# Cross attention with a scan on one core: row maxima taken over every fourth query and moved to rows by DMA, and the output projection run three groups ahead

## The chip, the cores and the metric

The kernel runs on one core of a Trainium2 chip. The metric is the device time of one execution in microseconds; the kernel before takes 2360.32 us, the median of 3 runs (2359.78 to 2363.59).

## What is computed

One transformer block with 4096 queries (x, 512 features) and 3202 keys (ctx), all in fp32. Cut to what matters:

```python
x  = layernorm(builder_state, g1, beta1)
kv = layernorm(base_state, g1, beta1)
q, k, v = heads of x @ Wq.T + bq, kv @ Wk.T + bk, kv @ Wv.T + bv      # 8 heads of 64
out = softmax(q @ k.T / 8) @ v
x = builder_state + out @ W_o.T + b_o
U = (layernorm(x, g2, beta2) @ W_in.T + b_in) @ Bmat
s = silu(s @ A.T) + u_t          # for every t, giving states
x = x + states @ Cmat
return x + (program_probs.mean(axis=1) @ W_prog.T + b_prog)
```

## The kernel before

Five engines each run a list of instructions written out by hand; semaphores join them. PE does the matmuls, ScalarE the exponentials and copies, VectorE the maxima and sums from PSUM, GpSimd (POOL) sums of the exponentials, and SP issues almost all DMAs, in one queue that also waits. On SP a wait holds up every DMA behind it.

**Precision.** q, k, O and W_o are split into a high part in fp32r and a low part, and a product is three passes. The maxima use the high parts alone.

**Stages.** Projection of q to DRAM (`q_scratch`) and of k and v, to 325 us; the attention, to 2121 us; the output projection with the second layernorm and U, to 2284 us; the scan and its output, to 2359 us.

**The attention** is cut into 32 units, one for each block of 512 queries and each pair of heads (`unit(w)`). A unit has 26 tiles of 128 keys, taken two at a time in 13 steps (`j`). In a step PE does, in this order: one of the maxima of a later unit (line 1136 or 1141); the shift for the even tile, a matmul of `ones_row` with `sh` (line 1230); the scores of both tiles (lines 1238, 1240, 1242); a second one of the maxima; PV of the two tiles before (line 1263). Every matmul here is a pair, one on the upper and one on the lower 64 rows of the array (or columns, for PV), for the two heads; the two run together. The shift subtracts the row maximum before the exponential. The even tile gets it on PE, the odd one on VectorE, which adds `shb` to PSUM (line 959).

**The maxima.** `maxima(w, m, i)` multiplies 128 queries of `qh` (the stationary operand) with 512 keys, so that a query is a partition and VectorE can reduce over the keys (`take_max`, lines 886 and 889). A unit has 26 of them: 24 with 512 keys, and two with the last 130 keys of two query tiles each (line 1141). `maxima_of` deals them out: 34 in unit 0, then two in a step, so that those of unit u + 1 end in step 8 of unit u. `row_max` (line 896) then reduces them to one maximum for each query and head in `mxp`. But `sh` and `shb` want the maxima along the free dimension. So PE transposes `mxp` in four pieces (`turn_max`, line 1150) in step 9, ScalarE copies the two rows, negated, to `sh` (`shift`, line 676), and SP stores them to `m_scratch` and loads them from there to all partitions of `shb` (`spread_shift`, lines 353 and 356).

**The output projection** has 16 groups of 256 queries. `project(d, t)` (line 1327) multiplies a tile of `og`, loaded by SP (`load_og`), with `wo_hl`, into bank 2 + t of PSUM; VectorE adds `xb` and takes the layernorm's statistics (`project` on VectorE), ScalarE normalises into `xn` (`norm2`), PE transposes (`turn2`, line 1336) and multiplies with `w_u` (`finish`, line 1348). PE runs two groups ahead: it projects group d + 2 before it transposes group d. `og` has two slots. The last unit's O goes through this stage late: its sum over keys (`spread_sum`, `take_den`, `fold_den`, `invert`, `spread_rden`), its scaling (`scale_o`, `high_o`, `low_o`) and its store (`store_o`) stand between the groups, and SP waits for each of them in its one queue. Groups 14 and 15 need that O.

**The scan** (line 1384) has as its moving operand `su` at every sixteenth column.

## Time and profile before

| | |
|---|---|
| median of 3 runs | 2360.32 us |
| the profiled execution | 2361.04 us |
| its span | 2358.9 us |
| PE busy | 2280.1 us, 97% |
| weight loads (PEld) busy | 1322.0 us, 56% |
| VectorE, GpSimd, ScalarE busy | 73%, 67%, 48% |
| share of PE in the chain that ended last | 91% |
| granted clock of PE over the execution | 0.978 |

In the views of the trace, PE stands for matmuls and PEld for the loads of their stationary operands, which can run beside a matmul before them. A form such as 64*128 64x512 is a matmul on 64 rows and 128 columns of the array, with 512 columns streamed. Matmuls are pipelined, so that the sum of their durations is more than the time in which PE is busy. SPq is SP issuing a DMA, and the time beside it is the time to issue it, not to move the data.

### The profile page before, as it was taken

What the parts mean: (1) busy time and instruction counts of PE and PEld (TensorE: products, weight loads), DVE (VectorE), ACT (ScalarE), POOL (GpSimd) and SP (SyncE); (2) the same over time, 40 slices, a digit from 0 to 9 for tenths busy, and PEclk for the clock granted to TensorE, in tenths of its full rate; (3) what the DMA queues carried; (4) which work ended last, traced back from release to release, by engine and by line L of the source; (5) the groups of instructions that cost most, each with busy time, mean ns of one, the idle gap of its engine ahead of it and who ended that gap; (6) DMA issues with size and microseconds to landing.
All of it is one profiled execution on the core that took longest, in us unless ns stands there. A gap on an engine that the chain in (4) does not pass through costs nothing.

```text
span 2358.9 us, 35969 instructions
## 1 busy us (share of the span) xinstructions
PE 2280.1 (97%) x14148; PEld 1322.0 (56%) x14148; DVE 1726.2 (73%) x2167; ACT 1121.5 (48%) x1429; POOL 1583.0 (67%) x1039
## 2 busy tenths in 40 slices
PE   8999989999999999999999999999999999998787
PEld 8998854555555545555555555555555555446553
DVE  5865446888888878888888878888877888646645
ACT  3654424444444444444544445444445444542354
POOL 1200026888888888888888888888888888883211
PEclk8999989999999999999999999999999999999887
DMA  6650225677777777777777777667777776775623
GB/s 242 216 175 10 81 75 120 151 156 157 157 154 160 169 168 171 174 156 159 164 161 166 178 171 166 154 154 155 160 157 157 156 159 155 183 175 152 198 77 143
DMA packets 158678, 365.01 MB, mean 155 GB/s; under 512 B 22511, under 2 KB 62063, under 8 KB 157870
## 3 DMA queue, kind: packets, MB, share of 16 engines
q0 software_dynamic: 59904, 218.13, 45.3%
q1 hardware_dynamic: 98606, 144.58, 18.9%
q8 instruction: 112, 1.84, 0.3%
q14 instruction: 56, 0.46, 0.1%
HBM read 95.41 MB, written 49.02 MB: 61 GB/s over the span
## 4 chain that ended last, share of the span: by engine, by line
PE 91%; DMA 3%; DVE 3%; ACT 1%; issue 1%; POOL 1%; SPq 0%; ACTq 0%; DVEq 0%; POOLq 0%
PE ps L1263 32%; PE ps L1136 11%; PE ps L1238 8%; PE ps L1240 8%; PE ps L1242 8%; PE ps L1230 4%; PE ps L1100 4%; PE ps L1118 3%; PE ps L1108 3%; PE ps L1327 3%; DMA acca<-pt 2%; PE ps L1384 1%; PE ps L1081 1%; PE ps L1273 1%; DVE mx_part L886 1%
## 5 line engine op out<-in xcount | busy, mean ns | idle before, releaser
L702 ACT ACTIVATE pt<-ps 128x1024 f32<-128x1024 f32 x800 | 779.2, 1021 | 911.5 <-PE ps L1242 889.5
L886 DVE TENSOR_REDUCE mx_part<-ps 128x2 f32<-128x1024 f32 x768 | 938.6, 1222 | 350.9 <-PE ps L1136 350.9
L520 POOL TENSOR_TENSOR accp<-accp,pt 128x1024 f32<-128x1024 f32 x416 | 1035.8, 2490 | 236.3 <-ACT pt L702 233.0
L1263 PE MATMUL ps<-pt,v 128*64 128x512 f32 x3328 | 807.0, 606 | 0.0
L959 DVE TENSOR_TENSOR ps<-ps,shb 128x1024 f32<-128x1024 f32 x403 | 493.2, 1224 | 50.5 <-PE ps L1242 50.5
L1263 PEld LDWEIGHTS ps<-pt,v 128*64 128x64 f32 x3328 | 202.2, 136 | 345.7 <-issue 338.5
L1136 PE MATMUL ps<-kk,qh 64*128 64x512 f32 x1536 | 350.6, 451 | 9.6 <-DVE mx_part L886 9.6
L1136 PEld LDWEIGHTS ps<-kk,qh 64*128 64x128 f32 x1536 | 143.6, 184 | 367.6 <-DVE mx_part L886 267.3
L1238 PE MATMUL ps<-qh,kk 64*128 64x512 f32 x1664 | 330.0, 391 | 3.9 <-ACT pt L702 3.9
L1242 PE MATMUL ps<-ql,kk 64*128 64x512 f32 x1664 | 330.1, 390 | 0.0
L1240 PE MATMUL ps<-qh,kk 64*128 64x512 f32 x1664 | 330.0, 391 | 0.0
L530 POOL DMA_DIRECT2D acca<-pt x192 | 182.3, 950 | 3.3 <-ACT pt L702 2.0
L1238 PEld LDWEIGHTS ps<-qh,kk 64*128 64x128 f32 x1664 | 157.8, 185 | 38.9 <-ACT pt L702 5.8
L1240 PEld LDWEIGHTS ps<-qh,kk 64*128 64x128 f32 x1664 | 158.4, 185 | 34.5
L1242 PEld LDWEIGHTS ps<-ql,kk 64*128 64x128 f32 x1664 | 158.4, 185 | 34.1
L1230 PE MATMUL ps<-sh,ones_row 64*128 64x512 f32 x858 | 173.9, 401 | 0.9 <-ACT pt L702 0.9
L509 POOL MEMSET sh<- 128x512 f32 x2 | 1.0, 530 | 187.2 <-PE ps L1118 187.2
L540 POOL DMA_DIRECT2D accb<-pt x128 | 125.7, 982 | 0.1
L1327 PE MATMUL ps<-wo_hl,og 128*128 128x512 f32 x384 | 100.0, 417 | 25.8 <-DMA og<-o_scratch 24.8
L1327 PEld LDWEIGHTS ps<-wo_hl,og 128*128 128x128 f32 x384 | 75.5, 201 | 48.2 <-DMA og<-o_scratch 27.0
L565 POOL TENSOR_TENSOR xb<-xb,bo 128x512 f32<-128x512 f32 x32 | 40.6, 1319 | 84.2 <-DMA xb<-x 84.2
L1230 PEld LDWEIGHTS ps<-sh,ones_row 64*128 64x128 f32 x858 | 82.6, 187 | 15.0 <-ACT pt L702 12.3
(150 smaller groups left out, 1933.5 us busy)
## 6 DMA issues: line engine op xcount, KB each, us to landing
acca<-pt POOLq DMA_DIRECT2D x224, 512.0 KB, 4.9
accb<-pt POOLq DMA_DIRECT2D x160, 512.0 KB, 4.8
q_scratch<-kk SPq DMA_DIRECT2D x32, 512.0 KB, 4.5
acca<-accp POOLq DMA_DIRECT2D x32, 512.0 KB, 4.6
o_scratch<-ost SPq DMA_DIRECT2D x32, 512.0 KB, 3.0
og<-o_scratch SPq DMA_DIRECT2D x32, 512.0 KB, 5.5
shb<-m_scratch SPq DMA_DIRECT2D x31, 512.0 KB, 4.2
xs<-x SPq DMA_DIRECT2D x16, 512.0 KB, 6.3
```

Source lines behind the costliest of these rows:

```text
L520: nc.gpsimd.tensor_tensor(acc[:, :], acc[:, :], pt[n % PT_SLOTS][:, :], ALU.add).then_inc(added_p, 1)
L530: nc.gpsimd.dma_start(acc[:, :], pt[n % PT_SLOTS][:, :], accum_op=ALU.add).then_inc(added_a[u % 2], 16)
L702: nc.scalar.activation(pt[n % PT_SLOTS][:, :], src, ACT.Exp, scale=SCALE).then_inc(exped, 1)
L886: nc.vector.tensor_reduce(mx_part[:, m % QT, :, m // QT], src, AX_X, ALU.max).then_inc(max_taken, 1)
L959: nc.vector.tensor_tensor(ps[:, b:b + 2, :], ps[:, b:b + 2, :], shb[u % 2][:, :, :], ALU.add)\
L1136: ins = mm(ps[:, bank, :], q[r, (m % QT) * P:(m % QT + 1) * P], kk[r, p, 0, a:a + QB], start=True, stop=True)
L1230: ins = mm(ps[:, 2 * (t % 2) + h, :], ones_row[r, :], sh[u % 2][r, :], start=first, stop=not first)
L1238: mm(ps[:, b + h, :], kk[r, p, 0, key], qh[u % 3][r, :], start=first, stop=False)
L1240: mm(ps[:, b + h, :], kk[r, p, 1, key], qh[u % 3][r, :], start=False, stop=False)
L1242: ins = mm(ps[:, b + h, :], kk[r, p, 0, key], ql[u % 2][r, :], start=False, stop=last)
L1263: ins = mm(ps[HD * h:HD * (h + 1), 6, :], v[:, t, f:f + HD], pt[n % PT_SLOTS][:, h * QB:(h + 1) * QB], start=(t == 0), stop=(t == NT - 1))
L1327: ins = mm(ps[:, 2 + t, :], og[:, d % 2, a, k, rows], wo_hl[:, b, k], start=(i == 0), stop=(i == len(PASSES) - 1))
```

## The change

It has two parts.

1. The maxima of `maxima(w, m, i)` are over queries `m % 4`, `m % 4 + 4`, ... (`q[r, m % QT:QB:QT]`) and no longer over 128 neighbouring ones; so partition p holds queries 4p to 4p + 3. For units 1 to 31 `row_max` writes a tile `mx_row` of 128 x 2 x 4, a second VectorE instruction negates it to `shift_col`, and SP stores that to `m_scratch` (each partition two pieces of 16 bytes), loads two rows of it into `sh`, and then `shb` as before. The transposes and ScalarE's copy stay for unit 0 only.
2. The output projection runs three groups ahead and `og` has three slots. The work on the last unit's O moves: on PE, ScalarE earlier (`spread_sum` and `take_den` at d = 0 for 2, `high_o` at 6 for 8), on GpSimd later (`scale_o` 10 for 8, `low_o` 12 for 10), on SP later (`fold_den` 6 for 4, `spread_rden` 9 for 6, `store_o` 13 for 10). The third slot lies where `wo_raw` was, so that its first load waits for `bo_mm` and `wo_lo`.

```diff
             def spread_shift(w):
                 sp.wait_ge(shift_ready, w + 1)
-                sp.dma_start(m_scratch[w % 2], sh[w % 2][0:HD + 1:HD, :].bitcast(F32)).then_inc(sh_stored, 16)
+                sp.dma_start(m_scratch[w % 2].rearrange("h (p t) -> p h t", t=QT), shift_col[:, :, :].bitcast(F32))\
+                    .then_inc(sh_stored, 16)
                 sp.wait_ge(sh_stored, 16 * w)
+                sp.dma_start(sh[w % 2][0:HD + 1:HD, :].bitcast(F32), m_scratch[w % 2]).then_inc(sh_loaded, 16)
                 wait(sp, shifted, tiles_added(w - 1))
...
             for d in range(2, X_G):
-                sp.wait_ge(y_done, GT * (d - 1))
-                if d % 2 == 0:
-                    sp.wait_ge(o_stored, 16 * (UNITS - BLOCKS + d // 2 + 1))
-                load_og(d)
+                if d >= OG_SLOTS:
+                    sp.wait_ge(y_done, GT * (d - OG_SLOTS + 1))
+                    if d % 2 == 0:
+                        sp.wait_ge(o_stored, 16 * (UNITS - BLOCKS + d // 2 + 1))
+                    load_og(d)
                 sp.wait_ge(x1_ready, GT * (d - 1))
                 load_x2(d)
-                if d == 4:
+                if d == 6:
                     fold_den(UNITS - 1)
-                if d == 6:
-                    spread_rden(UNITS - 1)
...
-                if d == 10:
+                if d == 9:
+                    spread_rden(UNITS - 1)
+                if d == 13:
                     store_o(UNITS - 1)
...
             def row_max(w):
                 dve.wait_ge(max_taken, NM * (w + 1))
-                wait(dve, max_turned, w)
-                nc.vector.tensor_reduce(mxp[:, :, 0:HD + 1:HD], mx_part[:, :, :, :], AX_X, ALU.max).then_inc(max_ready, 1)
-
+                wait(dve, sh_stored, 16 * (w - 1))
+                nc.vector.tensor_reduce(mx_row[:, :, :], mx_part[:, :, :, :].rearrange("p t h k -> p h t k"), AX_X, ALU.max).then_inc(max_ready, 1)
+                dve.wait_ge(max_ready, w + 1)
+                nc.vector.tensor_scalar(shift_col[:, :, :], mx_row[:, :, :], -1.0, None, ALU.mult).then_inc(shift_ready, 1)
...
-                        ins = mm(ps[:, bank, :], q[r, (m % QT) * P:(m % QT + 1) * P], kk[r, p, 0, a:a + QB],
+                        ins = mm(ps[:, bank, :], q[r, m % QT:QB:QT], kk[r, p, 0, a:a + QB],
                                  start=True, stop=True)
...
-                            ins = mm(ps[:, bank, i * TAIL_N:(i + 1) * TAIL_N], q[r, qt * P:(qt + 1) * P],
+                            ins = mm(ps[:, bank, i * TAIL_N:(i + 1) * TAIL_N], q[r, qt:QB:QT],
                                      kk[r, p, 0, TAIL:KEYS], start=True, stop=True)
...
-                if t == 0:
-                    pe.wait_ge(shift_ready, u + 1)
+                if t == 0 and u == 0:
+                    pe.wait_ge(shift_ready, 1)
+                if t == 0 and u > 0:
+                    pe.wait_ge(sh_loaded, 16 * u)
...
-                    if ahead and j == turn_step(u):
-                        turn_max(u + 1)
...
-                if d + 2 < X_G:
-                    project(d + 2, 1)
+                if d + OG_SLOTS < X_G:
+                    project(d + OG_SLOTS, 1)
                 turn2(d)
-                if d == 2:
+                if d == 0:
                     spread_sum(UNITS - 1)
```

PE's order in step 9 of a unit before, from the scores of the even tile on (line 1238, 1240, 1242 are the passes of the scores; 1150 the transposes, 1136 a maximum, 1263 PV):

```order
L1230 MATMUL ps<-sh_69,ones_row 128x512 x2
L1238 MATMUL ps<-qh_65,kk 128x512 x2
L1240 MATMUL ps<-qh_65,kk 128x512 x2
L1242 MATMUL ps<-ql_67,kk 128x512 x2
L1238 MATMUL ps<-qh_65,kk 128x512 x2
L1240 MATMUL ps<-qh_65,kk 128x512 x2
L1242 MATMUL ps<-ql_67,kk 128x512 x2
L1150 MATMUL ps<-ident,mxp 65x128 x4
L1136 MATMUL ps<-kk,qh_64 128x512 x2
L1263 MATMUL ps<-pt_71,v 64x512 x2
```

The same place in the changed kernel, whose lines are some nine further down:

```order
L1239 MATMUL ps<-sh_69,ones_row 128x512 x2
L1247 MATMUL ps<-qh_65,kk 128x512 x2
L1249 MATMUL ps<-qh_65,kk 128x512 x2
L1251 MATMUL ps<-ql_67,kk 128x512 x2
L1247 MATMUL ps<-qh_65,kk 128x512 x2
L1249 MATMUL ps<-qh_65,kk 128x512 x2
L1251 MATMUL ps<-ql_67,kk 128x512 x2
L1144 MATMUL ps<-kk,qh_64 128x512 x2
L1272 MATMUL ps<-pt_71,v 64x512 x2
```

The four transposes are gone and the maximum follows the scores directly, as in every other step.

SP's queue for one unit before (the denominators of the unit before, the shifts of the next unit, the store of O):

```order
L361 DMA den_80<-den_sb 64x1x8 x2
L366 DMA r_scratch<-rden_81 128x8
L370 DMA rdenb<-r_scratch 64x512 x2
L353 DMA m_scratch<-sh_69 2x512
L356 DMA shb_83<-m_scratch 128x1024
L413 DMA o_scratch<-ost 128x2x512
```

and in the changed kernel:

```order
L362 DMA den_80<-den_sb 64x1x8 x2
L367 DMA r_scratch<-rden_81 128x8
L371 DMA rdenb<-r_scratch 64x512 x2
L352 DMA m_scratch<-shift_col 128x2x4
L355 DMA sh_69<-m_scratch 2x512
L357 DMA shb_83<-m_scratch 128x1024
L414 DMA o_scratch<-ost 128x2x512
```

The store has another form, and the load of `sh` stands between it and the load of `shb`.

PE's order at the start of the output projection before:

```order
L1327 MATMUL ps<-wo_hl,og 128x512 x72
L1336 MATMUL ps<-ident,xn 128x128 x8
L1327 MATMUL ps<-wo_hl,og 128x512 x24
L1336 MATMUL ps<-ident,xn 128x128 x8
L1327 MATMUL ps<-wo_hl,og 128x512 x12
L1348 MATMUL ps<-nt,w_u 64x256 x8
```

and in the changed kernel:

```order
L1333 MATMUL ps<-wo_hl,og 128x512 x96
L1342 MATMUL ps<-ident,xn 128x128 x8
L1281 MATMUL ps<-acca_87,ones 64x512 x2
L1333 MATMUL ps<-wo_hl,og 128x512 x24
L1342 MATMUL ps<-ident,xn 128x128 x8
L1333 MATMUL ps<-wo_hl,og 128x512 x12
```

Four groups are projected before the first transposes in place of three (24 matmuls are a group), and the sum of the last unit follows these transposes directly.

## Rows read from the trace of the kernel before

**Rows 1.** The page, part 1: busy time of each engine.

```profile
PE 2280.1 (97%) x14148; PEld 1322.0 (56%) x14148; DVE 1726.2 (73%) x2167; ACT 1121.5 (48%) x1429; POOL 1583.0 (67%) x1039
```

**Rows 2.** Windows by stage: us, busy of PE, PEld, DVE, ACT, POOL, clock, DMA, GB/s.

```profile
383.00:2050.00 1667.00, 1661.87 (x10470) 848.40 (x10468) 1338.78 (x1226) 818.60 (x897) 1402.81 (x895) 1.00 0.72 161
2121.00:2284.00 163.00, 132.07 (x648) 100.28 (x648) 97.96 (x312) 57.42 (x98) 49.38 (x39) 0.91 0.49 154
```

**Rows 3.** Windows of two steps, PE alone, the first with the transposes.

```profile
1212.29:1217.22 4.93, 4.93 (x33) 1.00 0.74 138
1217.22:1221.35 4.13, 4.13 (x28) 1.00 0.60 156
```

**Rows 4.** Timeline of the weight loads in a step: start, length in us.

```profile
1204.06 0.19 PEld L1136 LDWEIGHTS ps<-kk,qh 64*128 64x128 f32 x2 [0.81 <-DVE mx_part L886]
1204.17 0.19 PEld L1230 LDWEIGHTS ps<-sh,ones_row 64*128 64x128 f32 x2
...
1205.55 0.19 PEld L1242 LDWEIGHTS ps<-ql,kk 64*128 64x128 f32 x2
1205.88 0.19 PEld L1136 LDWEIGHTS ps<-kk,qh 64*128 64x128 f32 x2
```

**Rows 5.** Timeline of VectorE in that unit.

```profile
1204.60 1.23 DVE L886 TENSOR_REDUCE mx_part<-ps 128x2 f32<-128x1024 f32 x1 [0.54 <-PE ps L1136]
...
1211.53 0.21 DVE L896 TENSOR_REDUCE mxp<-mx_part 128x8 f32<-128x56 f32 x1
1212.90 1.23 DVE L886 TENSOR_REDUCE mx_part<-ps 128x2 f32<-128x1024 f32 x1 [1.15 <-PE ps L1136]
```

**Rows 6.** Timeline of the weight loads, the last step of a set.

```profile
1208.21 0.30 PEld L1141 LDWEIGHTS ps<-kk,qh 64*128 64x128 f32 x4 [0.81 <-DVE mx_part L886]
...
1209.91 0.43 PEld L1141 LDWEIGHTS ps<-kk,qh 64*128 64x128 f32 x4
```

**Rows 7.** Windows in the scan, columns as in rows 2.

```profile
2290.00:2295.00 5.00, 4.84 (x19) 2.41 (x18) 0.00 (x0) 3.33 (x10) 0.00 (x0) 0.50 0.00 0
2315.00:2320.00 5.00, 4.84 (x19) 1.70 (x18) 3.02 (x5) 3.40 (x9) 0.00 (x0) 1.00 0.00 0
```

**Rows 8.** Groups of 2315:2320 us (first row), then single lines (min/median/max ns).

```profile
L1384 PE MATMUL ps<-su,at_sb 128*64 128x128 f32 x19 | 5.1, 398 | 0.2
...
L1348 PE MATMUL ps<-nt,w_u x128: 379/379/687, 2151.9 to 2283.8; 128*64 128x256 f32 x128
...
L1336 PE MATMUL ps<-ident,xn x128: 270/272/475, 2140.3 to 2279.7; 128*128 128x128 f32 x128
...
L1018 DVE TENSOR_REDUCE cb_sum<-cb_sb x1: 2931/2931/2931, 2227.1 to 2227.1; 128x64 f32<-128x1664 f32 x1
```

**Rows 9.** The page, part 5: busy, mean ns, idle before and releaser.

```profile
L1327 PE MATMUL ps<-wo_hl,og 128*128 128x512 f32 x384 | 100.0, 417 | 25.8 <-DMA og<-o_scratch 24.8
```

**Rows 10.** Timeline of SP, the shifts of one unit.

```profile
1216.89 0.51 SPq L353 DMA_DIRECT2D m_scratch<-sh  x1
1218.49 0.33 SPq L356 DMA_DIRECT2D shb<-m_scratch  x1
```

**Rows 11.** The page, part 6: KB each, us from issue to landing.

```profile
og<-o_scratch SPq DMA_DIRECT2D x32, 512.0 KB, 5.5
```

**Rows 12.** Timeline of PE in the output projection.

```profile
2165.93 8.22 PE L1327 MATMUL ps<-wo_hl,og 128*128 128x512 f32 x24 [7.21 <-DMA og<-o_scratch]
...
2187.66 7.33 PE L1327 MATMUL ps<-wo_hl,og 128*128 128x512 f32 x24 [4.18 <-DMA og<-o_scratch]
...
2230.20 8.53 PE L1327 MATMUL ps<-wo_hl,og 128*128 128x512 f32 x24 [9.42 <-DMA og<-o_scratch]
...
2248.20 5.72 PE L1327 MATMUL ps<-wo_hl,og 128*128 128x512 f32 x24
...
2278.14 1.97 PE L1336 MATMUL ps<-ident,xn 128*128 128x128 f32 x8 [3.64 <-ACT xn L743]
```

**Rows 13.** Timeline of SP in the output projection.

```profile
2160.56 1.14 SPq L418 DMA_DIRECT2D og<-o_scratch  x2
```

More of the change, by code:

```diff
@@ L32 @@
 X_SLOTS = 8
+OG_SLOTS = 3
 QB = 512
@@ L199, in build @@
         mxp = at("mxp", [P, QT, HD + 1], RR + 11776)
+        mx_row = at("mx_row", [P, 2, QT], 2576)
+        shift_col = at("shift_col", [P, 2, QT], 2584, F32R)
         mx_part = at("mx_part", [P, QT, 2, 7], RR + 12040)
@@ L298, in build @@
         bvb_ready = sem("bvb_ready"); bo_mm = sem("bo_mm"); bo_ready = sem("bo_ready")
-        og_loaded = [sem("og_loaded_0"), sem("og_loaded_1")]; x2_loaded = [sem("x2_loaded_0"), sem("x2_loaded_1")]
+        og_loaded = [sem(f"og_loaded_{i}") for i in range(OG_SLOTS)]; x2_loaded = [sem("x2_loaded_0"), sem("x2_loaded_1")]
         xb_ready = sem("xb_ready"); y_done = sem("y_done"); x1_ready = sem("x1_ready")
@@ L587, in _ @@
                 add_bias(d)
-                if d == 8:
+                if d == 10:
                     scale_o(UNITS - 1)
-                if d == 10:
+                if d == 12:
                     low_o(UNITS - 1)
@@ L669, in _, with first_shift @@
                     high_k(g, 3)
-            def shift(w):
-                act.wait_ge(max_turned, w + 1)
-                if w == 0:
-                    act.wait_ge(ones_set, 3)
-                nc.scalar.activation(sh[w % 2][0:HD + 1, :], ps[0:HD + 1, 7, :], ACT.Copy, scale=-1.0)\
-                    .then_inc(shift_ready, 1)
+            def first_shift():
+                act.wait_ge(max_turned, 1)
+                act.wait_ge(ones_set, 3)
+                nc.scalar.activation(sh[0][0:HD + 1, :].rearrange("r (p t) -> r p t", t=QT),
+                                     ps[0:HD + 1, 7, :].rearrange("r (t p) -> r p t", t=QT), ACT.Copy, scale=-1.0)                    .then_inc(shift_ready, 1)
             def exp_tile(u, t):
@@ L717, in high_o @@
                 nc.scalar.activation(ost[:, 0], oraw[:, :], ACT.Copy).then_inc(o_hi, 1)
-            shift(0)
+            first_shift()
             for u in range(UNITS):
@@ L729, in _ @@
                         high_o(u - 1)
-                    if j == turn_step(u) and u + 1 < UNITS:
-                        shift(u + 1)
                     if u == UNITS - 2 and j in (3, 5, 7, 9):
@@ L1140, in maxima, with first_turn @@
                             qt = 2 * (m - (NM - 2)) + i
-                            ins = mm(ps[:, bank, i * TAIL_N:(i + 1) * TAIL_N], q[r, qt * P:(qt + 1) * P],
+                            ins = mm(ps[:, bank, i * TAIL_N:(i + 1) * TAIL_N], q[r, qt:QB:QT],
                                      kk[r, p, 0, TAIL:KEYS], start=True, stop=True)
                 ins.then_inc(max_done, 1)
-            def turn_max(w):
-                pe.wait_ge(max_ready, w + 1)
-                wait(pe, den_taken, w - 1)
+            def first_turn():
+                pe.wait_ge(max_ready, 1)
                 for q in range(QT):
@@ L1269, in spread_sum @@
                 pe.wait_ge(added_a[u % 2], 16 * (len(A_TILES) + 1) * (u // 2 + 1))
-                if u + 1 < UNITS:
-                    pe.wait_ge(shift_ready, u + 2)
+                wait(pe, den_taken, u)
                 for h in (0, 1):
@@ L1326, in project @@
                 for i, (k, a, b) in enumerate(PASSES):
-                    ins = mm(ps[:, 2 + t, :], og[:, d % 2, a, k, rows], wo_hl[:, b, k],
+                    ins = mm(ps[:, 2 + t, :], og[:, d % OG_SLOTS, a, k, rows], wo_hl[:, b, k],
                              start=(i == 0), stop=(i == len(PASSES) - 1))
@@ L1353, in _ @@
             pe.wait_ge(bo_ready, 1)
-            for d in (0, 1):
+            for d in range(OG_SLOTS):
                 project(d, 0)
@@ L1357, in _ @@
             for d in range(X_G):
-                if d + 2 < X_G:
-                    project(d + 2, 0)
+                if d + OG_SLOTS < X_G:
+                    project(d + OG_SLOTS, 0)
                 if d > 0 and d % 2 == 0:
                     finish(d // 2 - 1)
-                if d + 2 < X_G:
-                    project(d + 2, 1)
+                if d + OG_SLOTS < X_G:
+                    project(d + OG_SLOTS, 1)
                 turn2(d)
-                if d == 2:
+                if d == 0:
                     spread_sum(UNITS - 1)
-                if d == 9:
+                if d == 8:
                     pe.wait_ge(cb_summed, 1)
```

31 lines of the change are left out of this document (18 added, 13 removed).

## The prediction

> **What bounds the kernel now.** I read the page's busy shares first, then its chain of waits, then windows by stage, then single steps of the attention in the timeline. PE is busy 2280.1 us, 97% of the span [rows 1], and the chain that ended last runs over PE nearly all the time. So time comes off only where PE does less or waits less, and anything that makes PE's own work longer is paid in full. By stage [rows 2]: from 383 to 2050 us (units 1 to 30 of the attention) PE is busy 1661.9 of 1667 us, at full clock: nothing is waited for there. From 2121 to 2284 us (the output projection) it is busy 132 of 163 us, at a granted clock of 0.91: there are some 31 us of waiting. The change touches both stages.
>
> The profiled execution took 2361.04 us, 2.1 more than its span and 0.7 above the median of the three runs (2360.32). The sum is made against 2361.0. I count a change of 0.2% (4.7 us) as the least that a measurement of this kernel tells from none.
>
> **Part 1: the transposes go.** A step with the four transposes lasts 4.93 us, the next one without them 4.13 [rows 3]: 0.80 us for each of 31 units, and since PE is the bound it is all gain: **-24.8 us**. ScalarE's copy into sh goes too; it is worth nothing, as ScalarE is busy 48% of the span [rows 1].
>
> **Part 2: the new way of the maxima.** VectorE gets one more small instruction per unit beside a reduction of 0.21 us, and it then sits idle 1.15 us before its next work [rows 5]: nothing. If that idle time were not there, it would cost 31 x 0.2 = 6 us. On SP's queue the store changes its form (128 partitions x 2 pieces of 16 bytes) and a load of two rows into sh is put between it and the load of shb. In the trace the old store is issued at 1216.89 and SP passes the wait for it at 1218.49, so 1.6 us in all [rows 10]. The new store and the new load are bounded by that 1.6 us below, and above by the 5.5 us of a load of 512 KB [rows 11]: 3 to 11 us together. I take 5. PE wants sh at the start of the next unit, four steps of 4.1 us after the row maximum (at 1211.7): 16 us. So it is in time at either end, and shb with it, since store and load now start at 1212 and not at 1217. Behind that wait on SP stands only the store of O, which was behind one already. Nothing.
>
> **Part 3: every fourth query as the weights.** This is the term that decides. The stationary operand of each matmul for the maxima was 128 consecutive columns of qh; now it is every fourth, 16 bytes apart. No weight load in this trace reads with a step, so its price must be bounded. Lower bound: nothing. Upper bound from the nearest rows: the scan's matmuls (line 1384) stream 128 elements that lie 64 bytes apart. At full clock they take 398 ns on average, where 128 consecutive elements take 272 ns and 256 consecutive ones 379 [rows 8]. And PE finishes 19 of them in 5 us at clock 0.50 and also 19 at clock 1.00 [rows 7], where eight transposes with consecutive operands take 1.97 us at the low clock [rows 12] against half of that at the high one. So a stepped operand of 32 bits seems to come at half the rate, whatever the clock. VectorE shows it too: cb_sum reads 1664 elements 256 bytes apart in 2.93 us, 1.76 ns each [rows 8], against 1.23 us for 1024 consecutive ones, 1.20 ns each [rows 5].
>
> The Trainium skill (SBUF — State Buffer, "Door 1: The DMA port swizzle") speaks against this change: it says that SBUF has lines of 16 bytes, that full rate needs at least two hits in a line, and that each access to a new line pays. Every fourth fp32 is a new line each time. The same paragraph then says that for fp32 a step of 4 is still free. By its first half the term is the one below, by its second half it is zero; the rows above, with far longer steps, cannot part the two at exactly 16 bytes.
>
> I take the upper bound, twice the time, since two engines show it. Now the size. A weight load of 128 columns holds the path for 0.11 us (starts at 1204.06 and 1204.17 [rows 4]); doubled, 0.22. The first load of maxima in a step stands right behind PV, cannot start ahead and is wholly exposed: +0.11. The second starts at 1205.88. The load before it started at 1205.55, and matmul pairs are 0.23 us apart, so its own matmul could start at 1206.01; it would be ready at 1206.10 in place of 1205.99: +0.09, so with the rounding some 0.19 us per step. (It starts where the first reduction, 1204.60 + 1.23, is done [rows 5], and that reduction moves back with the first matmul, so VectorE absorbs none of it.) In the last step of a set there are four loads for short matmuls, 0.30 and 0.43 us [rows 6], nothing to hide behind: +0.44. After the first unit there are 772 maxima, two in a step, so 386 steps: 356 x 0.19 + 30 x 0.44 = 67.6 + 13.2 = 80.8 us. The 34 maxima of unit 0 and 26 in the projections of K add about 60 x 0.09 = 5. **+86 us**, with 0 as the lower end.
>
> **Part 4: the output projection.** PE waits 24.8 us for og there [rows 9]. Three stalls make most of it, and each one leaves the clock low, so that the 24 projections behind it take 8.22, 7.33 and 8.53 us where 5.72 is normal [rows 12]: 6.9 us more. The stalls are not og's own transfer but what stands ahead of it on SP: og is issued at 2160.56 [rows 13] right after SP waited for the denominators of the last unit; the others follow the reciprocals and the store of the last O. The change puts these three later on SP (d = 6, 9, 13 for 4, 6, 10), their producers earlier on PE and ScalarE (d = 0), and gives og a third slot, so that a load of 5.5 us [rows 11] is issued about two loops before PE wants it. Gain 24.8 + 6.9 = 31.7. Against it: the last loops without a projection wait for ScalarE's xn, 3.64 us in the one shown [rows 12]; there is one more such loop: 3.6. Some 2 us for the copies into c1 and c2, which now stand in front of that wait. The bank: project(3, 0) needs VectorE to have emptied project(2, 0), so being three ahead doesn't fill the banks any deeper. I take **-26 us**; between -32 and -15, if one stall of 10 us stays.
>
> **Sum.** 2361.0 - 24.8 + 86 - 26 = **2396 us**.
>
> **Rivals.**
> *A, the forecast: stepped weights at half rate, exposed.* 60%. Its own range, from 70 to 95 us for the term and 18 to 30 for part 4, is 2376 to 2412.
> *B, the stepped load costs nothing* (the line's second-half rule above, or a weight path that fetches ahead). For it: no row shows a step of exactly 16 bytes, nor a stepped weight load. Against: two engines slow down with steps. Then 2361.0 - 24.8 - 26 = 2310 us. This is the faster side; it decides from the point where the term is below 51 us, that is below 0.12 us for a step. 27%.
> *C, half exposed*: only the first load of a step shows, the second hides in the 0.09 us which it now waits for VectorE: 386 x 0.11 + 30 x 0.22 + 3 = 52 us, so 2361.0 + 52 - 51 = 2362 us, no change. 10%.
> *D, the way through DRAM comes late.* If store, load and issue took more than the 16 us, PE would stand at the start of each unit, 31 us for each us too late, on top of any of the above. For it: 256 pieces of 16 bytes, which no row here shows. Against: five us at the least in hand by the bounds above. 3%.
>
> **The numbers.** The likeliest is A, 2396. B alone holds more than 2 in 10, so the range has to reach it: 2308 to 2408. Faster by over 0.2%: B and a little of C, 0.29. Within 0.2%: the middle of C, 0.06. Slower: A, D and the rest of C, 0.65.
>
> **What would show it.** Weight loads of the maxima of some 0.29 us in place of 0.18, steps of 4.3 us in place of 4.13, the same length in every step of a unit but the last of a set (4.5), and PE still busy without a gap: A. Loads of 0.18 us and steps of 4.13 throughout: B, and I am wrong by 86 us. For part 4: no wait over 2 us for og, the clock high throughout, the stage 137 us long in place of 163. If og is still waited for, the third slot was not what was short. For D: PE idle before the first shift matmul of a unit, released by the load of sh.

## The result and the profile after

The changed kernel takes **2445.48 us** (median of 4 runs, 2442.4 to 2447.16) beside 2360.05 us for the kernel before on the same chip: a ratio of 1.0358 [1.0345, 1.0371], 85 us slower. The forecast was 2396 with a range of 2308 to 2408. The direction was right and the size was not: 49 us more than forecast, 37 us above the upper end of the range.

| | before | after |
|---|---|---|
| span of the profiled execution | 2358.9 | 2443.7 |
| attention | 1797.1 | 1881.5 |
| output projection | 163.4 | 161.5 |
| a usual step of the attention | 4.13 to 4.15 | 4.36 to 4.37 |
| granted clock over the execution | 0.978 | 0.977 |

The attention runs from its first matmul to the first one of the output projection (323.76 to 2120.83 us, and 325.82 to 2207.33), the output projection from there to the end of its last matmul. The attention took 84.4 us more, what stands before it 2.1 more, the output projection 1.9 less, the scan 0.2 more: 84.8, all of the span's growth.

The page of the changed kernel, parts 1 and 4, to be read beside [rows 1]:

```profile
PE 2361.2 (97%) x14024; PEld 1415.7 (58%) x14024; DVE 1790.0 (73%) x2198; ACT 1110.4 (45%) x1398; POOL 1580.9 (65%) x1039
...
PE 87%; DVE 8%; issue 2%; ACT 1%; DMA 1%; POOL 0%; SPq 0%; ACTq 0%; POOLq 0%; DVEq 0%
PE ps L1272 29%; PE ps L1144 14%; PE ps L1247 7%; PE ps L1251 7%; PE ps L1249 7%; PE ps L1108 4%; PE ps L1239 4%; PE ps L1126 3%; PE ps L1116 3%; PE ps L1333 2%; DVE mx_part L889 2%; DVE shift_col L905 2%; PE ps L1390 1%; DVE ps L967 1%; PE ps L1089 1%
```

PE has 124 matmuls fewer (31 x 4 transposes) and is busy 81 us longer, with 94 us more of weight loads. That is the forecast mechanism. But VectorE now holds 8% of the chain, and one line of it is `shift_col L905`, a negation of 8 elements per partition, which the forecast had priced at nothing. It stands on the chain with 2% of the span.

Windows of the changed kernel, columns as in [rows 2]. The first three are one step each, from one first shift matmul to the next: the last of a set of maxima, the step behind the row maximum, a usual one. The fourth is the output projection.

```profile
1195.77:1200.17 4.40, 4.40 (x31) 2.71 (x32) 3.85 (x5) 1.94 (x2) 3.10 (x3) 1.00 0.84 181
1200.17:1205.23 5.06, 4.64 (x28) 2.34 (x26) 4.39 (x4) 2.05 (x2) 3.93 (x3) 1.00 0.65 118
1205.23:1209.60 4.37, 4.37 (x28) 2.34 (x26) 3.49 (x3) 2.46 (x3) 3.69 (x4) 1.00 0.74 195
2207.33:2368.85 161.52, 134.37 (x650) 100.55 (x648) 104.71 (x312) 57.64 (x98) 49.59 (x39) 0.91 0.52 156
```

In the second window a step that has lost its four transposes lasts 5.06 us, longer than the 4.93 that it took with them [rows 3]. PE is idle 0.42 us in it (5.06 less the 4.64 busy).

**The loads.** Timeline of the weight loads in two places of that unit (start, length, and the idle time before with what ended it):

```profile
1202.35 0.31 PEld L1144 LDWEIGHTS ps<-kk,qh 64*128 64x128 f32 x2 [0.85 <-DVE mx_part L889]
...
1204.77 0.31 PEld L1144 LDWEIGHTS ps<-kk,qh 64*128 64x128 f32 x2 [0.81 <-DVE mx_part L889]
1204.97 0.21 PEld L1239 LDWEIGHTS ps<-sh,ones_row 64*128 64x128 f32 x2
1205.23 0.19 PEld L1247 LDWEIGHTS ps<-qh,kk 64*128 64x128 f32 x2
```

The load of the maxima takes 0.31 us where it took 0.19, and the next one starts 0.20 us behind it where it started 0.11 behind [rows 4]: the path is held for twice as long. Loads of consecutive columns (L1247) still take 0.19.

**The negation.** Timeline of VectorE and, in the second fence, of GpSimd around the row maximum:

```profile
1198.83 0.21 DVE L903 TENSOR_REDUCE mx_row<-mx_part 128x8 f32<-128x56 f32 x1
1199.07 2.10 DVE L905 TENSOR_SCALAR shift_col<-mx_row 128x8 fp32r<-128x8 f32 x1
1201.08 1.21 DVE L889 TENSOR_REDUCE mx_part<-ps 128x2 f32<-128x1024 f32 x1
```

```profile
1198.77 2.37 POOL L526 TENSOR_TENSOR accp<-accp,pt 128x1024 f32<-128x1024 f32 x1 [1.30 <-ACT pt L707]
1201.09 0.86 POOL L536 DMA_DIRECT2D acca<-pt  x1
```

The negation starts at 1199.07 and ends at 1201.17; GpSimd's running sum, begun 0.30 us before it, ends at 1201.14. The reduction of the same 128 x 8 outputs right before it took 0.21 us while the same sum was running. The next reduction of maxima is thereby held until 1201.08, and PE's next maximum waits for the bank until 1202.35: the load of it waits the 0.85 us above, and PE itself is idle for 0.42 of them. Of the 31 negations 30 take 2.09 or 2.10 us. The view of this line gives the shortest, the median and the longest in ns:

```profile
L905 DVE TENSOR_SCALAR shift_col<-mx_row x31: 171/2095/2098, 382.4 to 2133.3; 128x8 fp32r<-128x8 f32 x31
```

The one of 171 ns is the first, and it is the one that no sum stood beside. GpSimd's sum before it ends at 382.34, and the negation starts 0.07 us later:

```profile
379.97 2.37 POOL L526 TENSOR_TENSOR accp<-accp,pt 128x1024 f32<-128x1024 f32 x1 [3.13 <-ACT pt L707]
```

```profile
382.41 0.17 DVE L905 TENSOR_SCALAR shift_col<-mx_row 128x8 fp32r<-128x8 f32 x1
```

The Trainium skill (SBUF — State Buffer, "SBUF: two separate sides") has the mechanism: VectorE and GpSimd share one pair of ports as an exclusive lock, which a VectorE instruction takes in its two-port mode or, beside a GpSimd instruction that reads SBUF, when both its inputs are in SBUF, and whichever engine comes second is blocked for the whole instruction of the other. By that rule the negation can't end before GpSimd's instruction does, and the trace agrees: it ends 0.03 us behind it. In which mode an instruction ran is in no view.

**The output projection.** PE's groups there in the changed kernel, beside [rows 9] (busy, mean ns, idle before, releasers):

```profile
L1333 PE MATMUL ps<-wo_hl,og 128*128 128x512 f32 x384 | 99.4, 416 | 19.7 <-DVE x_first L1010 11.5 <-DVE x_last L1010 8.2
```

Nothing waits for `og` any more. 24.8 us of waiting for a DMA has become 19.7 us of waiting for VectorE's sum into x. Why VectorE is late is in three timelines of the changed kernel, of ScalarE, VectorE and PE:

```profile
2238.89 1.51 ACT L746 ACTIVATE xn<-x_first,small 128x512 f32<-128x512 f32 x2
```

```profile
2235.84 1.35 DVE L1010 TENSOR_TENSOR x_first<-ps,xb 128x512 f32<-128x512 f32 x2
2240.50 1.28 DVE L852 BATCH_NORM_STATS2 small<-x_first 128x6 f32<-128x512 f32 x2 [3.30 <-ACT xn L746]
```

```profile
2223.09 13.38 PE L1333 MATMUL ps<-wo_hl,og 128*128 128x512 f32 x48 [4.59 <-DVE x_first L1010]
...
2246.44 2.97 PE L1333 MATMUL ps<-wo_hl,og 128*128 128x512 f32 x12 [1.53 <-DVE x_first L1010]
...
2264.19 4.44 PE L1333 MATMUL ps<-wo_hl,og 128*128 128x512 f32 x12 [2.74 <-DVE x_first L1010]
...
2283.45 2.96 PE L1333 MATMUL ps<-wo_hl,og 128*128 128x512 f32 x12 [2.66 <-DVE x_first L1010]
...
2301.91 4.57 PE L1333 MATMUL ps<-wo_hl,og 128*128 128x512 f32 x12 [3.44 <-DVE x_last L1010]
```

VectorE has the sum of a group at 2237.2, but starts its statistics only at 2240.50, when ScalarE's `xn` of an older group has ended (2240.40). Behind them stands the next group's sum, which is what empties the bank for PE. The reason is a wait that the change left alone: the layernorm's scale and bias have two slots, so `project(d)` on VectorE waits for `normed2` of group d - 2 before it may write them. PE now runs three groups ahead, so that normalisation has itself to wait for transposes that stand behind a projection on PE. And after some of these waits the granted clock is low: 12 matmuls take 4.44 or 4.57 us there, at a granted clock of 0.63, where others take 2.97 and 2.96, at 1.00.

### The profile page after: what moved, and what is told of

It is laid out like the page before. It is cut to its first block, busy times and chain, and to the rows that moved or that the text cites. A ratio compares the mean times of both kernels' runs of the same rounds, so it can differ in the third digit from the quotient of the medians.

```text
span 2443.7 us, 35692 instructions
## 1 busy us (share of the span) xinstructions
PE 2361.2 (97%) x14024; PEld 1415.7 (58%) x14024; DVE 1790.0 (73%) x2198; ACT 1110.4 (45%) x1398; POOL 1580.9 (65%) x1039
## 4 chain that ended last, share of the span: by engine, by line
PE 87%; DVE 8%; issue 2%; ACT 1%; DMA 1%; POOL 0%; SPq 0%; ACTq 0%; POOLq 0%; DVEq 0%
PE ps L1272 29%; PE ps L1144 14%; PE ps L1247 7%; PE ps L1251 7%; PE ps L1249 7%; PE ps L1108 4%; PE ps L1239 4%; PE ps L1126 3%; PE ps L1116 3%; PE ps L1333 2%; DVE mx_part L889 2%; DVE shift_col L905 2%; PE ps L1390 1%; DVE ps L967 1%; PE ps L1089 1%
## 5 line engine op out<-in xcount | busy, mean ns | idle before, releaser
L526 POOL TENSOR_TENSOR accp<-accp,pt 128x1024 f32<-128x1024 f32 x416 | 1024.8, 2463 | 320.8 <-ACT pt L707 318.8
L1144 PEld LDWEIGHTS ps<-kk,qh 64*128 64x128 f32 x1536 | 237.4, 306 | 386.9 <-DVE mx_part L889 290.4
L1144 PE MATMUL ps<-kk,qh 64*128 64x512 f32 x1536 | 435.8, 563 | 21.8 <-DVE mx_part L889 21.8
L1247 PE MATMUL ps<-qh,kk 64*128 64x512 f32 x1664 | 330.9, 393 | 0.6 <-ACT pt L707 0.6
L1247 PEld LDWEIGHTS ps<-qh,kk 64*128 64x128 f32 x1664 | 157.9, 185 | 35.4 <-ACT pt L707 1.2
L546 POOL DMA_DIRECT2D accb<-pt x128 | 118.7, 927 | 0.0
L1333 PE MATMUL ps<-wo_hl,og 128*128 128x512 f32 x384 | 99.4, 416 | 19.7 <-DVE x_first L1010 11.5
L1239 PEld LDWEIGHTS ps<-sh,ones_row 64*128 64x128 f32 x858 | 89.6, 205 | 16.0 <-ACT pt L707 14.1
```

The source lines that it names most:

```text
L526: nc.gpsimd.tensor_tensor(acc[:, :], acc[:, :], pt[n % PT_SLOTS][:, :], ALU.add).then_inc(added_p, 1)
L1144: ins = mm(ps[:, bank, :], q[r, m % QT:QB:QT], kk[r, p, 0, a:a + QB], start=True, stop=True)
L1239: ins = mm(ps[:, 2 * (t % 2) + h, :], ones_row[r, :], sh[u % 2][r, :], start=first, stop=not first)
L1247: mm(ps[:, b + h, :], kk[r, p, 0, key], qh[u % 3][r, :], start=first, stop=False)
L1333: ins = mm(ps[:, 2 + t, :], og[:, d % OG_SLOTS, a, k, rows], wo_hl[:, b, k], start=(i == 0), stop=(i == len(PASSES) - 1))
```

## The experiments

All kernels below compute the whole output. The kernel before was run beside each; its median was between 2360.1 and 2363.0 us.

**1. Each part alone.** First, part 2 of the change in the kernel before (three slots of `og`, three groups ahead, the moved steps), and no part 1:

```diff
+OG_SLOTS = 3
...
-        og = at("og", [P, 2, 2, FC, GW], 6656, F32R)
+        og = at("og", [P, OG_SLOTS, 2, FC, GW], 6656, F32R)
...
             def project(d, t):
-                pe.wait_ge(og_loaded[d % 2], 32 * (d // 2 + 1))
+                pe.wait_ge(og_loaded[d % OG_SLOTS], 32 * (d // OG_SLOTS + 1))
```

> The kernel before with part 2 of the change alone (three groups ahead, three slots for og, the last unit's O moved); maxima as before. Theory 1 (the stepped weight loads, the negation on VectorE and a projection that gained nothing together make the loss): from the traces the projection lasts 161.5 us in the changed kernel against 163.4 before, so 2361 - 2 = 2359 us, no change; no wait for og, but seven or eight waits of 1.4 to 4.6 us for VectorE's sum into x. Theory 2 (the projection did gain the 26 us that I forecast, and the maxima cost all the more): 2335 us.

Measured: 2357.02 us (10 runs), ratio 0.9983 [0.9973, 0.9993]. Its profile has the waits of the changed kernel, in the same places:

```profile
L1333 PE MATMUL ps<-wo_hl,og 128*128 128x512 f32 x384 | 98.1, 412 | 17.3 <-DVE x_first L1008 12.6 <-DVE x_last L1008 4.6
```

So the second part is worth 3 us, not 26. What it removes is there (no wait for `og`), and is given back.

Second, part 1 alone (the changed kernel with its output projection put back):

```diff
-OG_SLOTS = 3
...
-        og = at("og", [P, OG_SLOTS, 2, FC, GW], 6656, F32R)
+        og = at("og", [P, 2, 2, FC, GW], 6656, F32R)
...
-                if d == 0:
+                if d == 2:
                     take_den(UNITS - 1)
```

> The kernel before with part 1 of the change alone; projection as before. Theory 1: 2445.5 + 2 = 2447 us, steps of 4.37 us, 5.06 in the step after the maxima of a unit. Theory 2: 2445.5 + 26 = 2471 us.

Measured: 2450.92 us, ratio 1.0384 [1.0366, 1.0401], with steps of 4.37 and 5.06 us as in the changed kernel. The parts add up to within 3 us: -3 and +91 against +85. (Put on top of the first part, the second is worth 5 us by the medians and 1 by the spans, 2444.9 and 2443.7.)

**2. The loads alone.** The kernel before, with only the stationary operand of the maxima changed and ScalarE's copy putting the rows back in order; transposes and everything else stay:

```diff
-                nc.scalar.activation(sh[w % 2][0:HD + 1, :], ps[0:HD + 1, 7, :], ACT.Copy, scale=-1.0)\
+                nc.scalar.activation(sh[w % 2][0:HD + 1, :].rearrange("r (p t) -> r p t", t=QT),
+                                     ps[0:HD + 1, 7, :].rearrange("r (t p) -> r p t", t=QT), ACT.Copy, scale=-1.0)\
...
-                        ins = mm(ps[:, bank, :], q[r, (m % QT) * P:(m % QT + 1) * P], kk[r, p, 0, a:a + QB],
+                        ins = mm(ps[:, bank, :], q[r, m % QT:QB:QT], kk[r, p, 0, a:a + QB],
```

> The kernel before with nothing changed but the queries of a maximum (every fourth) and, to match, the order in which ScalarE's copy reads the transposed maxima. Theory 1: weight loads of 0.31 us, steps of 4.37 us, 386 x 0.23 + 34 x 0.1 + 2 = 94 us more than before: 2454. By my forecast's size (0.19 for a step, 86 in all): 2446. Rival (part of the loss of the changed kernel that I put down to the loads comes with the way through DRAM): under 2430.

Measured: 2451.96 us, ratio 1.0384 [1.0365, 1.0402], span 2450.6. Group and windows (a step with the transposes, a usual one):

```profile
L1137 PEld LDWEIGHTS ps<-kk,qh 64*128 64x128 f32 x1536 | 237.3, 306 | 367.2 <-DVE mx_part L887 266.2
```

```profile
1203.30:1208.45 5.15, 5.15 (x34) 2.75 (x31) 3.59 (x3) 2.42 (x3) 4.03 (x3) 1.00 0.63 119
1208.45:1212.81 4.36, 4.36 (x28) 2.34 (x26) 3.49 (x3) 2.46 (x3) 3.62 (x4) 1.00 0.64 173
```

The span grows by 91.7 us from the loads alone; the reordered copy on ScalarE takes 590 ns for 592. And the two windows price the transposes under stepped loads: 5.15 - 4.36 = 0.79 us, as in the kernel before (0.80).

**3. The negation in another form.** My first reading of the 2.10 us was that the one-input instruction's fast mode takes the lock and an instruction with two tensor inputs would not. So -2m + m in place of -1 times m:

```diff
-                nc.vector.tensor_scalar(shift_col[:, :, :], mx_row[:, :, :], -1.0, None, ALU.mult).then_inc(shift_ready, 1)
+                nc.vector.scalar_tensor_tensor(out=shift_col[:, :, :], in0=mx_row[:, :, :], scalar=-2.0,
+                                               in1=mx_row[:, :, :], op0=ALU.mult, op1=ALU.add).then_inc(shift_ready, 1)
```

> The changed kernel with the negation written as a scalar_tensor_tensor (-2 * m + m) in place of a tensor_scalar of one operand. Theory 1 (the tensor_scalar stands until GpSimd's running sum is done, as the other tensor_scalars do in the output projection, and the two-operand form does not): the instruction takes 0.2 us and not 2.1, the step after it 4.37 us and not 5.06, so 2445.5 - 31 x 0.7 = 2424 us. Rival (VectorE waits for something else there, such as the store on SP or the write before): the instruction or the one behind it still takes 2 us, and the time stays at 2445.

Measured: 2446.1 us, ratio 1.0362 [1.0345, 1.0379], the same as the changed kernel.

```profile
1200.61 2.08 DVE L905 SCALAR_TENSOR_TENSOR shift_col<-mx_row 128x8 fp32r<-128x8 f32 x1
```

GpSimd's sum in this run started at 1200.30 and took 2.37, so it ended at 1202.67; the negation ended at 1202.69. That reading fell: one tensor input or two, the negation stands until GpSimd's end. The second case of the Trainium skill's rule above, two inputs in SBUF, fits this run as its first fits the changed kernel.

**4. No negation.** The reduction, which took 0.21 us beside the same GpSimd instruction, writes `shift_col` itself; the sign moves into the constants (`ones_row` is -1, VectorE subtracts `shb`). The rest is the changed kernel.

```diff
-                nc.vector.tensor_reduce(mx_row[:, :, :], mx_part[:, :, :, :].rearrange("p t h k -> p h t k"), AX_X, ALU.max).then_inc(max_ready, 1)
-                dve.wait_ge(max_ready, w + 1)
-                nc.vector.tensor_scalar(shift_col[:, :, :], mx_row[:, :, :], -1.0, None, ALU.mult).then_inc(shift_ready, 1)
+                nc.vector.tensor_reduce(shift_col[:, :, :], mx_part[:, :, :, :].rearrange("p t h k -> p h t k"), AX_X, ALU.max).then_inc(max_ready, 1)
...
-                nc.vector.tensor_tensor(ps[:, b:b + 2, :], ps[:, b:b + 2, :], shb[u % 2][:, :, :], ALU.add)\
+                nc.vector.tensor_tensor(ps[:, b:b + 2, :], ps[:, b:b + 2, :], shb[u % 2][:, :, :], ALU.subtract)\
```

> The changed kernel without the negation: the reduction of the row maxima writes shift_col itself, ones_row holds -1, and VectorE subtracts shb in place of adding it. Theory 1 (both tensor_scalar and scalar_tensor_tensor on SBUF stand until GpSimd's running sum ends, a tensor_reduce does not): the reduction takes 0.21 us, the step behind it 4.37 us in place of 5.06, so 2445.5 - 31 x 0.7 = 2424 us. Rival (the next maxima wait there for another reason, the write of shift_col or its store): the step stays at 5.06 and the time at 2445.

Measured: 2427.68 us, ratio 1.0278 [1.026, 1.0297]: 18 us less than the changed kernel (21 by the spans). The view of the reduction, and windows of the step behind the row maximum and of the next:

```profile
L903 DVE TENSOR_REDUCE shift_col<-mx_part x31: 210/211/211, 384.4 to 2117.2; 128x8 fp32r<-128x56 f32 x31
```

```profile
1194.23:1198.66 4.43, 4.43 (x28) 2.34 (x26) 3.49 (x3) 1.94 (x2) 3.31 (x3) 1.00 0.66 117
1198.66:1203.03 4.37, 4.37 (x29) 2.34 (x26) 3.49 (x3) 2.46 (x3) 4.36 (x4) 1.00 0.71 187
```

5.06 became 4.43 and PE has no idle time in it: 31 x 0.63 = 19.5 us. The negation was the missing term of part 2.

**5. Consecutive queries, so no stepped loads.** The changed kernel with 128 neighbouring queries again; the store to DRAM then falls into 1024 pieces of 4 bytes.

```diff
-                sp.dma_start(m_scratch[w % 2].rearrange("h (p t) -> p h t", t=QT), shift_col[:, :, :].bitcast(F32))\
+                sp.dma_start(m_scratch[w % 2].rearrange("h (t p) -> p h t", t=QT), shift_col[:, :, :].bitcast(F32),
+                             allow_slow_non_contiguous=True)\
...
-                        ins = mm(ps[:, bank, :], q[r, m % QT:QB:QT], kk[r, p, 0, a:a + QB],
+                        ins = mm(ps[:, bank, :], q[r, (m % QT) * P:(m % QT + 1) * P], kk[r, p, 0, a:a + QB],
```

> The changed kernel with the maxima over 128 consecutive queries again; the maxima still go to rows by DMA, in 1024 pieces of 4 bytes in place of 256 of 16. Theory 1 (the step of 16 bytes doubles the weight load): loads of 0.18 us and not 0.31, steps of 4.14 us, so 2445.5 - 386 x 0.23 = 2357 us, if the small pieces land in the 16 us that there are. Rival (the way through DRAM or its traffic slows the steps): the time stays over 2430 or grows with the smaller pieces; should the store come too late, PE waits at the start of each unit, 31 us for each us.

Measured: 2384.8 us, ratio 1.0108 [1.0089, 1.0127]. The loads are back at 183 ns and a usual step at 4.15 us, 61 us less than the changed kernel, but 28 more than I expected. Windows of the step behind the row maximum and of the next, and the group of ScalarE's exponentials from 383 to 2050 us in this run (first fence) and in the changed kernel (second):

```profile
1162.86:1167.93 5.07, 4.42 (x30) 2.10 (x27) 4.63 (x4) 2.05 (x2) 4.18 (x3) 1.00 1.11 129
1167.93:1172.08 4.15, 4.15 (x28) 2.13 (x26) 3.49 (x3) 2.32 (x3) 3.49 (x4) 1.00 0.73 29
...
L707 ACT ACTIVATE pt<-ps 128x1024 f32<-128x1024 f32 x737 | 723.0, 1022 | 864.3 <-PE ps L1251 781.2 <-DMA acca<-pt 60.8 <-DVE ps L967 20.4
```

```profile
L707 ACT ACTIVATE pt<-ps 128x1024 f32<-128x1024 f32 x711 | 694.6, 1022 | 888.8 <-PE ps L1251 871.4 <-DVE ps L967 13.3 <-DMA acca<-pt 4.1
```

Two things make up most of the rest. The wait for GpSimd costs more where steps are shorter: 5.07 - 4.15 = 0.92 us, 29 us in all, for the 21 that I had expected. And the store stands in the way of other DMAs: moving 4 KB, it is issued at 1164.13 and SP passes the wait for it at 1172.89, 8.8 us; in the second window, which lies in that stretch, no more than 29 GB/s are moved (194 in the like window of experiment 6, below). GpSimd's accumulating DMAs (`acca<-pt` in part 6 of the page) land after 5.3 us for 4.8, and ScalarE waits 60.8 us for them for 4.1. These are not SP's: SP does not issue almost all DMAs, as said of the kernel before; GpSimd issues 416 there, with 218 of the 365 MB. The changed kernel's longer steps give them more time; in the kernel before, with steps of the same length, ScalarE waits 14.2. PE waits 14.1 us for ScalarE, 11 more than before (2.7). Together 29 + 11 on 2361.0 - 24.8 - 2 give 2374, against 2380.4 for the profiled execution and 2384.8 for the median: 6 to 11 us stay open. The first negation of this run started 0.42 us before the end of GpSimd's sum (376.28) and took 0.45.

**6. Every second query.** From experiment 4, with a step of 8 bytes: a tile of 128 queries is every second one of 256. The store has 512 pieces of 8 bytes. Were the price that of a step as such, the loads would stay near 0.3 us; were it that of one element in 16 bytes, they would be free.

```diff
-                        ins = mm(ps[:, bank, :], q[r, m % QT:QB:QT], kk[r, p, 0, a:a + QB],
+                        ins = mm(ps[:, bank, :], q[r, 2 * P * (m % QT // 2) + m % 2:2 * P * (m % QT // 2 + 1):2], kk[r, p, 0, a:a + QB],
```

> As no_negation, but a tile holds every second query (steps of 8 bytes, two to a line of 16), and the maxima go to DRAM in 512 pieces of 8 bytes. Theory 1 with the line rule (two hits in a line are enough): weight loads of 0.18 us, steps of 4.14 us, 386 x 0.23 = 88 us less than no_negation, so 2336, and some 10 us back for the smaller pieces: 2336 to 2350. Rival (any step halves the rate): loads of 0.31 us and 2424 or more.

Measured: 2342.31 us, ratio 0.9922 [0.9902, 0.9943]: 85 us less than experiment 4, and faster than the kernel before. Group of the loads and windows as above:

```profile
L1143 PEld LDWEIGHTS ps<-kk,qh 64*128 64x128 f32 x1536 | 149.3, 191 | 368.2 <-DVE mx_part L890 278.4
```

```profile
1202.35:1206.54 4.19, 4.19 (x28) 2.11 (x26) 3.49 (x3) 1.94 (x2) 3.30 (x3) 1.00 0.75 128
1206.54:1210.70 4.16, 4.16 (x29) 2.11 (x27) 3.49 (x3) 2.34 (x3) 4.16 (x4) 1.00 0.71 194
```

191 ns at 8 bytes, 306 at 16, 183 for neighbours. So a step as such is not what costs. The number of elements that share 16 bytes explains these three, and so would a limit on the step anywhere from 8 to 16 bytes: no run has a step of 12, which would tell them apart. The store costs SP 5.4 us here (1201.48 to 1206.83), and PE never waits for it.

**7. The first load behind the shift.** From experiment 4: PE does the first maximum of a step behind the shift matmul, where its load can run beside another matmul, and not behind PV.

```diff
-                    for w, m in todo[:1]:
-                        maxima(w, m, m)
+                    if not added(u, 2 * j + 1):
+                        for w, m in todo[:1]:
+                            maxima(w, m, m)
...
                         shift_scores(u, 2 * j, True)
+                        for w, m in todo[:1]:
+                            maxima(w, m, m)
                         open_tile(u, 2 * j + 1)
```

> no_negation with the first maxima of a step put behind the shift matmul in place of ahead of it (stepped loads of 16 bytes kept). If the exposed 0.11 us is that the load stands directly behind PV: the load hides beside the shift's matmul and a step is 0.11 us shorter, 386 x 0.11 = 42 us less than no_negation: 2382. If VectorE's three operations pace the step then (its first reduction starts 0.1 us later): nothing gained, 2424, and the second maxima wait longer for VectorE.

Measured: 2462.18 us, ratio 1.0421 [1.0402, 1.044]; both expectations were far too low. Weight loads, then VectorE:

```profile
1199.96 0.31 PEld L1142 LDWEIGHTS ps<-kk,qh 64*128 64x128 f32 x2
...
1201.91 0.31 PEld L1142 LDWEIGHTS ps<-kk,qh 64*128 64x128 f32 x2 [0.39 <-DVE mx_part L889]
```

```profile
1200.63 1.23 DVE L889 TENSOR_REDUCE mx_part<-ps 128x2 f32<-128x1024 f32 x1 [0.88 <-PE ps L1142]
```

The first load does hide, beside a matmul. But its matmul comes 0.34 us into the step (1199.86 to 1200.20), VectorE's reduction of it starts 0.77 us into the step for 0.67 in experiment 4 and ends at 1201.86, and the load of the second maximum, which wants that reduction done, waits 0.39 us. Its matmul starts 0.35 us behind the one before it where 0.23 is usual, and PV 0.55 us behind that where experiment 4 has 0.43. (PE counts as busy throughout, as matmuls overlap and their ends are modelled.) Steps are 4.47 us for 4.37, 386 x 0.10 = 39 us against 34.5 measured. A hidden load was worth less than the turn it had to wait for. The second theory had the wait, but not that it costs more than the load.

**8. A third slot of the layernorm's scale and bias.** From the first kernel of experiment 1:

```diff
-        ya = small[:, 20:24].rearrange("p (s t) -> p s t", s=2)
+        ya = [small[:, 20:22], small[:, 22:24], small[:, 44:46]]
...
-                wait(dve, normed2, d - 1)
-                layernorm(d % 2, lambda t: x1(d)[:, t, :], ln2_ready)
+                wait(dve, normed2, d - 2)
+                layernorm(d % 3, lambda t: x1(d)[:, t, :], ln2_ready)
```

> proj_only with a third slot for the scale and bias of the second layernorm, so that VectorE waits for ScalarE's normalisation of group d - 3 and not of d - 2. Theory 1 (that wait is what gave the gain of the projection back): no wait of VectorE for xn, no waits of PE for the sum into x of over 1 us but the first (4.8), full clock in the middle; 17 us of waits and some 6 of low clock less: 2357 - 20 = 2337 us. Rival (the sum waits for xb, that is for the load of x and GpSimd's bias, two slots): PE still waits, 2355 us.

Measured: 2342.72 us, ratio 0.9921 [0.9899, 0.9944], 14 us less than without the slot. The group that had 17.3 us of waits:

```profile
L1333 PE MATMUL ps<-wo_hl,og 128*128 128x512 f32 x384 | 95.3, 403 | 7.3 <-DVE x_first L1008 5.3 <-DVE x_last L1008 2.0
```

10 us of waits went, and 2.8 of busy time, since the granted clock of the stage rose to 0.95. What is left is mostly one wait of 4.81 us near the stage's start, for VectorE's first sums. The 2337 us that I had expected were 6 us too low; `xb` and `xn`, with two slots and one, were left as they are.

**9. Both mended.** Experiments 6 and 8 in one kernel (its edits are theirs).

> every_second with the third slot for the second layernorm's scale and bias: maxima over every second query, no negation, three groups ahead with three slots of each. The parts lie in different stages and should add: 2342.3 - (2357.0 - 2342.7) = 2328 us, ratio 0.986 to the kernel before. If the projection is paced by xb or og once the attention feeds it otherwise: 2340.

Measured: **2327.04 us** (2323.96 to 2328.76), ratio 0.985 [0.9835, 0.9865]. It beats both kernels: 118 us under the changed one, 36 under the one before that ran beside it (2362.97).

## Why the prediction was right or wrong

| term | forecast | measured | from |
|---|---|---|---|
| part 1, transposes | -24.8 | -24.5 | 31 x 0.79, experiment 2 |
| part 2, negation | 0 | +18 to +21 | experiment 4 against the changed kernel |
| part 2, way through DRAM | 0 | 0 | no wait for `sh` |
| part 3, stepped loads | +86 | +92 | spans, experiment 2 |
| part 4, output projection | -26 | -2 to -3 | stage's length; experiment 1 |
| sum on 2361.0 | 2396 | 2443 to 2448 | measured 2445.5 |

**Part 1 held**: 0.80 us for a step forecast, 0.79 measured with stepped loads. No run removes the transposes alone. Experiment 4 is experiment 2 without them, with the way through DRAM and part 2 of the change; it is 24 us faster by the medians and 28 by the spans, of which 2 to 3 are the projection's. Both fit.

**Part 2 failed** at the sentence "VectorE gets one more small instruction ... nothing", and its hedge of 6 us failed with it. I priced the instruction by a neighbour of the same size, a reduction of 0.21 us [rows 5], and set it against an idle 1.15 us. It takes 2.10, since it waits for GpSimd's instruction to end, and that makes PE's step 0.63 us longer, 31 times. So most of what the transposes had given was taken back in the very step that lost them. The trace of before had shown it and I did not look there. In the very unit of [rows 5], a GpSimd sum begins 0.06 us before the row maximum (1211.53) and runs to 1213.85, 0.95 us past the start of VectorE's next work (1212.90), so the idle 1.15 us were not free for an instruction that it holds up:

```profile
1211.47 2.38 POOL L520 TENSOR_TENSOR accp<-accp,pt 128x1024 f32<-128x1024 f32 x1 [0.94 <-ACT pt L702]
```

That a sum can hold a small instruction up stood there too. Timeline of VectorE in the kernel before, at the second layernorm, two instructions of two elements per partition each:

```profile
2129.32 0.17 DVE L818 TENSOR_SCALAR small<-small 128x2 int32<-128x2 int32 x1
2129.53 2.29 DVE L819 TENSOR_SCALAR small<-small 128x2 int32<-128x2 int32 x1
```

and GpSimd there:

```profile
2129.39 2.40 POOL L546 TENSOR_TENSOR accp<-accp,accb 128x1024 f32<-128x1024 f32 x1
```

The one that started 0.07 us before GpSimd's took 0.17 us, the one that started 0.14 us behind it 2.29, ending 0.03 us behind it. The size of an instruction told nothing; the neighbour on the other engine did.

**Part 2's DMAs held.** `sh` and `shb` are issued by 1204.2, about 5 us behind the row maximum and 3 behind the negation, and PE never waits for them (rival D is out). The store of 256 pieces of 16 bytes costs SP 2.5 us (1201.19 to 1203.64). When the load of `sh` lands is in no view, so the 3 to 11 us for both are not checked beyond the missing wait.

**Part 3 held in mechanism** and was 6 us too small. The load holds the path for 0.20 us in place of 0.11, near the factor of two that was forecast, and the runs decide between the two halves of the paragraph in the Trainium skill that the prediction weighed. By the Trainium skill (SBUF — State Buffer, "Specifications (TRN2)") full rate needs at least two hits in a line of 16 bytes; experiments 2 and 6 agree, with 306 ns for one hit and 191 for two. Were every fourth fp32 free, as the paragraph's other half has it, the loads would have stayed near 183, and they did not. That the factor came out at two is in part luck, since the rows that it was taken from do not show it. VectorE's 1.76 ns against 1.20 is a factor of 1.5, and the 1.20 was read from PSUM. And the 19 matmuls in 5 us at either clock are paced by the scan's chain and not by their operand: in those windows ScalarE waits for each pair of matmuls and the next load waits for ScalarE, 0.43 us each time at the low clock. The size: 0.19 us per step forecast, 0.22 to 0.24 measured (4.13 to 4.15 became 4.36 to 4.37). The last step of a set, taken with both its short maxima (1208.21 to 1212.29 before, 1195.25 to 1199.71 after), grew by 0.38 (4.08 to 4.46), not 0.44. 356 x 0.22 + 30 x 0.38 = 90, with some 2 us ahead of the attention (2.1 measured, 5 forecast) 92.

**Part 4 failed**, by 23 us, the largest error of the four. It took the 24.8 us for `og` as gained because no other ring would be in the way: "being three ahead doesn't fill the banks any deeper". That is true of the banks and was the only ring I looked at. `og` got its third slot, `ya` and `nmr` kept two, and their wait on `normed2` took the place of the DMA's. I had followed the edits on SP's queue and PE's order, and not what stands unedited on VectorE's. Of the three signs that I named, "no wait over 2 us for og" came; the clock, "high throughout" by the forecast, was granted at 0.91 as before, and the stage, forecast at 137 us, took 161.5. Experiment 8 gave 14 us of the 23 back by one more slot. The other 9 are not settled in detail; 4.8 us of them is the wait at the stage's start, which no slot takes away.

**The rivals.** A came in its mechanism and not in its range (2376 to 2412, by its own terms 2413), since its sum took two gains as certain. B is out by the 306 ns, and C by steps that grew by 0.22 to 0.24 us where it has 0.11. D is out by the missing wait. That a small instruction could meet a lock was no rival at all, and it should have been: VectorE's 2.29 us above was its row.

**The sum.** Two of the four terms were wrong, both in the same direction, by some 20 and 23 us, and the loads' 6 us make up the 49. They share one fault: each was costed at what it does on its own engine, without asking what the other user of the same port, or the other ring in the same loop, would do.

## What to carry to other kernels

Before a transpose is replaced by a strided operand, choose the step such that at least two elements share 16 bytes: steps of 8 bytes left the usual step of the attention at 4.16 us (4.13 to 4.15 for neighbours), steps of 16 bytes cost 92 us in all. A small VectorE instruction from SBUF to SBUF beside long GpSimd work should be priced by what is left of the GpSimd instruction, not by its size, unless a row shows that its kind is not held (here the reduction was not, `tensor_scalar` and `scalar_tensor_tensor` were); fold it into a reduction or into a constant. And when a loop is made to run further ahead, list every ring that its stages share, the smallest ones of two columns too, and read which of them the next wait falls on: here a third slot of two columns was worth 14 us.

## What the hardware showed that was not expected

- A VectorE instruction of 8 elements per partition took 2.10 us beside a GpSimd sum of 2.37 us, in either of two forms, 0.17 where the sum had just ended and 0.45 where 0.42 us of it were left; a reduction (0.21 us) beside the same GpSimd instruction was not held.
- Weight loads of 128 fp32 columns: 183 ns for neighbours, 191 at a step of 8 bytes, 306 at 16.
- A DMA of 4 KB to DRAM held SP, from issue to the wait passed, for 2.5 us in 256 pieces of 16 bytes, 5.4 in 512 of 8, and 8.8 in 1024 of 4; the last also slowed others (landing 5.3 us for 4.8).
- Hiding a weight load can cost more than it saves, where it moves the producer of a later wait: +34 us in experiment 7.
